# First threshold and goal of the second step on GpSimd, fewer stages in VectorE's bracket update, ties marked once behind the repeat loop

## What is computed

```python
def _adj_from_feats(Xa, W1, W2, W3):
    logits = (Xa @ W1) @ W2 @ (Xa @ W3).T
    idx = jnp.argsort(-logits, axis=1)
    vals = jnp.take_along_axis(logits, idx, axis=1)
    csum = jnp.cumsum(jax.nn.softmax(vals, axis=1), axis=1)
    k_i = jnp.sum(csum < 0.9, axis=1) + 1            # how many are kept
    keep = ...                                       # the k_i largest of each row
    return jax.nn.softmax(jnp.where(keep, logits, -jnp.inf), axis=1)

for s in range(2):                                   # the two steps
    A = _adj_from_feats(Xa, W1, W2, W3)
    Xf, Xb, Xa = Rf @ Xf, Rb @ Xb, A @ Xa
    Z = Z + Xf @ U1[s] + Xb @ U2[s] + Xa @ U3[s]
```

## Time and profile before

| | |
|---|---|
| median of 3 runs | 2055.96 us (2055.61 to 2056.17) |
| the profiled execution | 2057.05 us, of which 2055.3 are its span from first to last instruction |
| busy in the span | TensorE 1783.8 us (87%), VectorE 1666.5 (81%), ScalarE 1365.6 (66%), GpSimd 554.8 (27%) |
| mean granted clock of TensorE | 0.954 of full speed |

### The profile page before, as it was taken

One profiled execution on the slowest core, in us unless ns is written; L12 is line 12 of the kernel. 1 busy time (PEld: TensorE's weight loads), 2 busy tenths in 40 slices (PEclk: granted clock), 3 DMA queues, 4 the chain that ended last, 5 costly groups with the idle time before them and its releaser, 6 DMA issues.

```text
span 2055.3 us, 37644 instructions
## 1 busy us (share of the span) xinstructions
PE 1783.8 (87%) x11660; PEld 1314.4 (64%) x11660; DVE 1666.5 (81%) x4215; ACT 1365.6 (66%) x2157; POOL 554.8 (27%) x869
## 2 busy tenths in 40 slices
PE   3999953899999999994956599999999999999997
PEld 3888831677777777773744366666666666666665
DVE  6444465899999999998871899999999999999996
ACT  5222266788888888883724677777777777777752
POOL 4000030344443444431331032222222222222220
PEclk9999977899999999997978799999999999999999
DMA  6899621444444444442424010101010101010122
GB/s 163 198 203 206 169 99 40 106 114 114 110 103 111 114 106 106 112 111 54 96 50 143 21 40 22 38 24 37 24 37 24 37 24 37 24 37 24 37 89 70
DMA packets 235346, 168.27 MB, mean 82 GB/s; under 512 B 188451, under 2 KB 220577, under 8 KB 235168
## 3 DMA queue, kind: packets, MB, share of 16 engines
q1 hardware_dynamic: 221264, 117.44, 21.1%
q0 software_dynamic: 3744, 22.14, 7.0%
q10 hardware_dynamic: 10288, 28.12, 4.0%
HBM read 107.99 MB, written 37.49 MB: 71 GB/s over the span
## 4 chain that ended last, share of the span: by engine, by line
DVE 46%; PE 19%; DVEq 17%; issue 10%; DMA 3%; ACT 3%; ACTq 0%; POOLq 0%; POOL 0%; SPq 0%
DVE probs_t L1529 7%; DVE stats L1546 5%; DVE stats L1536 5%; DVE window L1426 4%; DVEq L1727 4%; DVE scraps L1426 4%; DVE sorted_e L1555 2%; DVE window L1589 2%; DVEq L1593 2%; DVE expo L1409 2%; DMA probs_t<-astray 2%; DVEq L1553 2%; PE lg L1099 2%; PE bank L1035 2%; PE bank L1034 2%
## 5 line engine op out<-in xcount | busy, mean ns | idle before, releaser
L1122 PE MATMUL bank<-both,s_tile 128*128 128x512 f16 x1352 | 301.6, 380 | 16.1 <-issue 16.1
L1191 PE MATMUL bank<-xcur,probs_t 128*128 128x256 f32 x1352 | 296.1, 379 | 0.0
L1099 PE MATMUL lg<-k_t,q_tile 64*128 64x512 f32 (+1 forms) x820 | 192.9, 572 | 100.3 <-DVE expo L1409 92.0
L1191 PEld LDWEIGHTS bank<-xcur,probs_t 128*128 128x128 f32 x1352 | 254.9, 190 | 33.6
L639 POOL TENSOR_TENSOR window<-window,probs_t 128x832 f16<-128x832 f32 x104 | 223.1, 2145 | 113.4 <-ACT probs_t L876 100.8
L1122 PEld LDWEIGHTS bank<-both,s_tile 128*128 128x128 bf16 x1352 | 132.6, 98 | 165.3 <-issue 18.2
L1409 DVE TENSOR_SCALAR_CACHE_REDUCE expo<-lg 128x1024 f32 (+1 forms) x208 | 205.0, 1022 | 36.5 <-PE lg L1089 16.4
L818 ACT ACTIVATE expo<-expo,neg_max 128x3327 f32<-128x3327 f32 x52 | 159.4, 3066 | 47.0 <-DVE neg_max L1418 47.0
L1099 PEld LDWEIGHTS lg<-k_t,q_tile 64*128 64x128 f32 x820 | 69.9, 194 | 183.4 <-DVE expo L1409 120.1
L665 POOL TENSOR_TENSOR aims<-found 128x2 f32<-128x2 f32 x26 | 5.1, 196 | 623.4 <-ACT found L844 623.4
L839 ACT ACTIVATE turned<-expo,found 128x3327 uint8<-128x3327 f32 x52 | 159.7, 3072 | 3.6
(11 more groups left out here) (295 smaller groups left out, 3643.7 us busy)
## 6 DMA issues: line engine op xcount, KB each, us to landing
s_tile<-s_scratch SPq DMA_DIRECT2D x28, 832.0 KB, 4.5
expo<-in_adj POOLq DMA_DIRECT2D x25, 831.8 KB, 9.5
s_tile<-s_scratch ACTq DMA_DIRECT2D x24, 832.0 KB, 4.5
s_scratch<-s_tile SPq DMA_DIRECT2D x14, 832.0 KB, 9.7
s_scratch<-probs_t SPq DMA_DIRECT2D x6, 832.0 KB, 9.4
s_scratch<-window SPq DMA_DIRECT2D x6, 832.0 KB, 9.4
q_tile<-q_scratch SPq DMA_DIRECT2D x104, 32.0 KB, 2.1
xa_scratch<-ht ACTq DMA_DIRECT2D x26, 128.0 KB, 1.9
```

Of the source, the lines that this page charges most:

```text
L1099: last = T.matmul(lg[c % 2][:, h * CHUNK:h * CHUNK + w], q_tile[b][DA * h:DA * (h + 1), :], k_all[DA * h:DA * (h + 1), s, c0:c0 + w], star ...
L1122: last = T.matmul(s_ps[:, 0:width], s_tile[b][:, k, :], moving, start=(k == 0 and part == 0), stop=(k == NT - 1 and part == 1))
L1191: last = T.matmul(kept_ps[1][:, 0:D], probs_t[:, k * P:(k + 1) * P], xcur[:, k, :], start=(k == 0), stop=(k == NT - 1))
```

## The change

Three things, and sizes of buffers that go with them.

- GpSimd: `first_bracket` goes on to the first cut and its goal. Before, it left the difference of the values and that of the cuts times the upper value. Now it raises the first to the power of -1 (`ALU.pow`), multiplies the second by it, adds the lower end, works out the goal, and multiplies the goal with the four signs of `sides`. `lead` and `mine` get 16 columns for it.
- VectorE, second step: the reciprocal and the product behind L1650 and the goal in `evaluate` are gone. Which ends to replace is decided by comparing `sides` x sum with `sides` x goal, beside the difference rather than behind it. The two instructions of `settle` stand beside the reciprocal's stages; `interpolate` and `settle` are part of `evaluate`.
- VectorE, repeat branch: in the first step the count of ties is taken out of the flag ahead of the loop, the entries equal to the threshold are made ready, and the flags are gathered again, so that the loop runs only if a row is flagged for something else. `take_ties` and `take_above` stand once behind the loop, in both steps.

```diff
@@ -193,8 +193,8 @@
         last_bias = acts[:, 7:8]
         sieved = sb("sieved", [P, 2])
 
-        mine = sb("mine", [P, 12])
-        lead = sb("lead", [P, 2, 12])
+        mine = sb("mine", [P, 16])
+        lead = sb("lead", [P, 2, 16])
         scalar_points = sb("scalar_points", [P, 4])
         aims = sb("aims", [P, 2])
         picked = sb("picked", [P, 2, 8])
@@ -206,14 +206,15 @@
         my_total = mine[:, 4:5]
         my_target = mine[:, 5:6]
         my_slack = mine[:, 6:7]
+        goal = mine[:, 3:4]
         bracket = mine[:, 8:12]
+        goal_by_side = mine[:, 12:16]
         ends_t = sb("ends_t", [P, 4])
         ends_c = sb("ends_c", [P, 4])
         sides = sb("sides", [P, 4])
         which = sb("which", [P, 8], I32)
         reach = sb("reach", [P, 2])
         weight = sb("weight", [P, 1])
-        goal = cells[:, 0:1]
         under = sb("under", [P, 1])
         settled = sb("settled", [P, 1], I32)
         ceiling = sb("ceiling", [P, 1])
@@ -224,6 +225,9 @@
         sorted_e = sb("sorted_e", [P, MOST])
         prefix = sb("prefix", [P, MOST + 1])
         mass = prefix[:, 0:1]
+        row_powers = sb("row_powers", [P, 2])
+        power = row_powers[:, 0:1]
+        below = row_powers[:, 1:2]
         ranks = sb("ranks", [P, 8])
         lists = [sieve[:, HALF - 3 * MOST:HALF], scraps[:, N - N % 4 - 12 * MOST:N - N % 4].bitcast(FP32)]
         equal = rest[:, BEST - 8:BEST]
@@ -239,7 +243,6 @@
         real_row = sb("real_row", [P, 1])
         top = cells[:, 7:8]
         kept = cells[:, 6:7]
-        below = sb("below", [P, 1])
         odd = sb("odd", [P, 32])
         odd_t = rest[:, 0:32]
         odd_q = sb("odd_q", [P, 1])
@@ -578,6 +581,7 @@
             G.memset(parts[:, :, 2 * D:2 * D + 2], 1.0)
             G.memset(zeros_bf[:, :], 0.0)
             G.memset(ceiling[:, :], CEILING)
+            G.memset(power[:, :], -1.0)
             for rank in range(8):
                 G.memset(ranks[:, rank:rank + 1], float(rank))
             for slot, (of_t, of_one, way) in enumerate(((0.0, 0.0, -1.0), (0.9, 0.0, 1.0), (0.0, CEILING, 1.0), (-0.1035, 0.0, -1.0))):
@@ -686,8 +690,16 @@
                     pool.drain()
                 G.tensor_tensor(span[:, :], lead[:, b, 10:12], lead[:, b, 8:10], ALU.subtract)
                 pool.drain()
-                G.tensor_copy(lead[:, b, 2:3], span[:, 1:2])
-                G.tensor_tensor(lead[:, b, 1:2], span[:, 0:1], lead[:, b, 11:12], ALU.mult).then_inc(lead_ready, 1)
+                G.tensor_tensor(span[:, 0:1], span[:, 0:1], lead[:, b, 11:12], ALU.mult)
+                G.tensor_tensor(span[:, 1:2], span[:, 1:2], power[:, :], ALU.pow)
+                pool.drain()
+                G.tensor_tensor(span[:, 0:1], span[:, 0:1], span[:, 1:2], ALU.mult)
+                pool.drain()
+                G.tensor_tensor(lead[:, b, 0:1], span[:, 0:1], lead[:, b, 8:9], ALU.add)
+                pool.drain()
+                G.tensor_scalar(lead[:, b, 3:4], lead[:, b, 0:1], AIM[1], lead[:, b, 6:7], ALU.mult, ALU.add)
+                pool.drain()
+                G.tensor_scalar(lead[:, b, 12:16], sides[:, :], lead[:, b, 3:4], None, ALU.mult).then_inc(lead_ready, 1)
             def centre_result(t, m, b):
                 pool.wait_ge(y_moments, t + 1)
                 y = tile3(y_all, tile_of(m, b))
@@ -1433,36 +1445,26 @@
                                       points[r].rearrange("p (a d) -> p a d", a=1).broadcast_to([P, 2, 2]))
                     dve.drain()
 
-                def interpolate():
-
+                def evaluate(b):
+
+                    mass_under(b, terms)
+                    dve.drain()
+                    V.tensor_tensor(point[:, 1:2], under[:, :], goal, ALU.subtract)
+                    V.scalar_tensor_tensor(out=which[:, 0:4], in0=sides[:, :], scalar=under[:, :], in1=goal_by_side,
+                                           op0=ALU.mult, op1=ALU.is_gt)
+                    dve.drain()
+                    replace_ends(0)
                     V.tensor_tensor(reach[:, :], bracket[:, 2:4], bracket[:, 0:2], ALU.subtract)
+                    V.scalar_tensor_tensor(out=under[:, :], in0=bracket[:, 2:3], scalar=AIM[s], in1=bracket[:, 1:2],
+                                           op0=ALU.mult, op1=ALU.add)
                     dve.drain()
                     V.reciprocal(weight[:, :], reach[:, 1:2])
                     V.tensor_tensor(reach[:, 0:1], reach[:, 0:1], bracket[:, 3:4], ALU.mult)
+                    V.scalar_tensor_tensor(out=settled[:, :], in0=bracket[:, 0:1], scalar=SETTLED, in1=under[:, :],
+                                           op0=ALU.mult, op1=ALU.is_ge)
                     dve.drain()
                     V.scalar_tensor_tensor(out=cut, in0=weight[:, :], scalar=reach[:, 0:1], in1=bracket[:, 0:1],
                                            op0=ALU.mult, op1=ALU.add)
-                    dve.drain()
-
-                def evaluate(b):
-
-                    V.tensor_scalar(goal, cut, AIM[s], my_slack, ALU.mult, ALU.add)
-                    mass_under(b, terms)
-                    dve.drain()
-                    V.tensor_tensor(point[:, 1:2], under[:, :], goal, ALU.subtract)
-                    dve.drain()
-                    V.tensor_scalar(which[:, 0:4], sides[:, :], point[:, 1:2], 0.0, ALU.mult, ALU.is_gt)
-                    dve.drain()
-                    replace_ends(0)
-                    interpolate()
-
-                def settle(b):
-
-                    V.scalar_tensor_tensor(out=weight[:, :], in0=bracket[:, 2:3], scalar=AIM[s], in1=bracket[:, 1:2],
-                                           op0=ALU.mult, op1=ALU.add)
-                    dve.drain()
-                    V.scalar_tensor_tensor(out=settled[:, :], in0=bracket[:, 0:1], scalar=SETTLED, in1=weight[:, :],
-                                           op0=ALU.mult, op1=ALU.is_ge)
                     dve.drain()
                     V.copy_predicated(cut, settled[:, :], bracket[:, 2:3])
                     dve.drain()
@@ -1650,17 +1652,10 @@
                         V.tensor_copy(mine[:, :], lead_of(b))
                     dve.drain()
                     if s == 1:
-                        V.reciprocal(weight[:, :], mine[:, 2:3])
-                        dve.drain()
-                        V.scalar_tensor_tensor(out=cut, in0=weight[:, :], scalar=mine[:, 1:2], in1=bracket[:, 0:1],
-                                               op0=ALU.mult, op1=ALU.add)
                         if not is_last(t):
                             copy_logits(t + 1, other, LOGITS_LATE)
-                        else:
-                            dve.drain()
                     if s == 1:
                         evaluate(b)
-                        settle(b)
                         dve.wait_ge(p_flipped, t * NG + 1)
                     else:
                         few(b)
@@ -1686,13 +1681,20 @@
 
                         dve.drain()
                         V.memset(tries, TRIES)
+                        if s == 0:
+                            V.tensor_tensor(astray[:, :], astray[:, :], tied, ALU.subtract)
+                            V.tensor_scalar(equal, ranks[:, :], tied, below[:, :], ALU.is_lt, ALU.mult)
+                            V.tensor_scalar(least, tied, 8.0, None, ALU.is_gt)
+                            dve.drain()
+                            V.tensor_tensor(astray[:, :], astray[:, :], least, ALU.add)
+                            dve.drain()
+                            find_odd(astray[:, :], t)
+                            dve.reg_load(left, odd_n[0:1, 0:1])
                         with dve.While(left):
                             move_cut(b)
                             rank(b)
                             flag(True)
                             dve.drain()
-                            take_ties(b)
-                            take_above(b, True, 0, N)
                             sum_kept()
                             find_odd(astray[:, :], t)
                             V.tensor_scalar(tries, tries, -1.0, None, ALU.add)
@@ -1701,6 +1703,9 @@
                                                    op1=ALU.mult)
                             dve.drain()
                             dve.reg_load(left, again)
+                        take_ties(b)
+                        take_above(b, True, 0, N)
+                        dve.drain()
                         dve.reg_load(left, odd_n[0:1, 0:1])
                         with dve.While(left):
                             climb(b)
```

## The result

The changed kernel took 2036.36 us (median of 4 runs, 2035.17 to 2037.08) against 2056.07 us of the kernel before beside it: 19.7 us between the medians, and a ratio of 0.9899 with a 95% interval of 0.9883 to 0.9915, which puts the gain at 17.5 to 24.1 us. The forecast was 2028.6 us, 27.4 faster; the time lies inside its range of 2017 to 2051, 7.8 us above its centre. The profiled execution has a span of 2034.7 us, against 2055.3 before, at a granted TensorE clock of 0.958 (mean of the span).

A forecast was written before the change was run, and what follows sets the result against it. VectorE was taken as the second step's bound, TensorE next. From 2057.05 us, 15.2 off for the second step and 12.2 for the repeats gave 2029.65; the runs' median being 1.09 lower, 2028.6, range 2017 to 2051.

The forecast's parts named there:

- three rivals: Cases the range takes in: both repeats real, 0.13; only the number of instructions counts, 0.05; pow of middling length, 0.12.
- The forecast case: Whole kernel: second step 15.2 us and repeats 12.2 us faster, 2018 to 2034 us of its own; chance 0.57.
- middling pow: Second step: pow of 0.7 to 1.4 us holds L1650, keeping only part of the gain, 2034 to 2051 us; chance 0.12.
- five signs of being right: L1180's wait 0.4 us or less, tile distance 33.7, L1650 0.3 to 0.6, repeat only in t=22, t=24 some 12.
- signs of being wrong: A repeat in t=24; VectorE waiting for the bracket each tile, or for late logits; pow over 0.7 us.
- The bound: Second step: VectorE's chain of instructions sets the pace, 34.36 us per tile, with TensorE next, 0.9 us behind.
- Part 3, the repeats: First step's repeat branch: t=22 real, +3.3 us; t=24 flagged for ties alone, -15.5 us; together -12.2 us.
- Part 1, bracket update: VectorE, second step: sides save 0.16 us and settling 0.31 us per tile through fewer drained distances.
- Part 1, taking over: VectorE, L1650 to the next copy of logits: 0.78 us falls to one drained distance of 0.24, saving 0.54 per tile.
- Part 1, goal: VectorE, second step: the goal (L1449) ahead of L1426 goes away, saving 0.12 us per tile.
- Part 2, pow and cover: GpSimd's bracket: +1.5 us, pow up to 0.5, 0.6 to 0.9 of cover left; centring over L1650 loses 0.45 per tile.
- Long pow: GpSimd: pow so long that the bracket becomes the bound, at 2.5 us +25.5, 2081 us; chance 0.10.

The follow-up runs named there:

- fewer stages alone: Kernel before with only interpolate and settle merged, settling's two instructions beside the reciprocal's stages, GpSimd's work as before; 2047.77 us, ratio 0.9958.
- the second pow: Changed kernel with another pow on GpSimd behind the first, its result unused; 2040.59 us, ratio 0.9915.

## Why the prediction was right, and which step of it was not

**How near it came.** The range of 2017 to 2051 holds the time, but it is that wide because it takes in three rivals. The forecast case alone was given 2018 to 2034, and 2036.4 lies above it, in the stretch of middling pow, which didn't happen. So the mechanism is the forecast one and the gain in the second step was put too high. Of the five signs of being right three came (the time of L1652 with the centring beside it, the repeat in t = 22 alone, 12 us in t = 24) and two came halfway (TensorE's wait at 0.50 instead of 0.4 or less, the period at 33.97 instead of 33.7). Of the signs of being wrong none came in full: the bracket is waited for in every second tile, not in each, and the only long row of pow is one that was held.

**The bound: right.** VectorE's chain of small stages set the second step's pace, with TensorE next. Shortening the chain shortened the period, and TensorE's wait for kept_inv shrank, from 0.87 to 0.50 us per tile; 0.4 or less was forecast for a gain of 0.65.

**Part 3, the repeats: right.** -15.3 and +2.3, forecast -15.5 and +3.3. Tile t = 24 was flagged for ties alone and t = 22 for something else, as forecast; which rows it was, no view shows. The microsecond too much has two parts. From L1683 to the loop's first instruction it is 2.85 us (943.39 to 946.24) and not 3.3, since the register load and the branch are 0.5, not 0.8. And the first counting pass of the second ranking took 1.95 us instead of 2.51 (L1531 at 948.38, before L1529 at 942.05); before, an addition of GpSimd (L644, 942.09 to 942.81) lay beside it, and now it was over by then; that this is the cause is likely and not shown. The half microsecond is luck.

**Part 1, bracket update: right.** Sides and settling were to save 0.47, and from L1452 to the second pass 0.50 went away, with both kinds of evidence: the kernel with fewer stages alone has the 0.34 of settling (forecast 0.31) without dropping an instruction, and the three drains put back cost 0.51 where they stand. "VectorE: DVE Perf Modes" of the Trainium skill says in its section on the DRAIN that the next operation does not start until the pipeline is empty, adding that one that isn't held starts earlier, and in "Rules for kernel authors" to minimize the number of operations rather than the semaphores (the prediction put that advice into the first section). For small operations that don't depend on each other the rows here agree with the addition and not with the rule, 0.08 against 0.24 us.

**Part 1, taking over: the step that failed.** "from L1650 to the next copy of logits (L1409) was 0.78 ...; one drained distance of 0.24 is left. Saved 0.54." It is 0.80, so nothing was saved. The two instructions are gone, but two other things took their place:
- The copy takes 0.46 instead of 0.17, because of the centring. The prediction had that as a term of its own, 0.45 lost, and it measured 0.29. "SBUF — State Buffer" of the Trainium skill, section "SBUF: two separate sides", has the lock as its rule; the trace agrees (L706 starts at 1498.17 and ends at 1498.78, L1652 starts at 1498.36 and ends at 1498.82, just behind it). The collision comes in nearly every tile because both instructions follow the bracket: once its cover is gone, GpSimd begins the centring as soon as the bracket is done, and VectorE the copy some 0.15 us later.
- Behind the copy's drain the copy of logits starts 0.34 us later. The price of 0.24 was taken from small instructions; this one's row in the profile has "issue" as its reason. The kernel with the centring moved, where the copy takes only 0.17, has the same 0.34 (L1653 at 1492.90, L1422 at 1493.42), and without the drain 0.13 is left (L1654 at 1492.95 plus 0.18, L1423 at 1493.26). So it belongs to the drain and not to the lock.
Both counted, the step should have read: 0.78 - 0.17 - 0.34 = 0.27 saved, 0.29 of it lost to the lock.

**Part 1, goal: half.** 0.12 forecast, 0.07 measured (neg_max to the first pass 0.18 before, L1418 to L1426, and 0.11 after, L1430 to L1438).

**Part 2, pow and cover: right in kind.** Pow was taken as up to 0.5 us and took 0.57; the long pass catches an earlier stage, as said: L691, one ahead of what it caught before, and in every second tile L689, two ahead. With 0.6 to 0.9 us of cover the forecast had no wait; there is 0.33 in every second tile, 0.16 per tile. The first bracket: +2.0 for the wait, forecast +1.5; most of the rest is pow, 0.57 instead of 0.2. Long pow and middling pow didn't happen. What the second pow cost (0.20 per tile for 0.55) says that the rival was right in that the cover does end there, and that its price, one for one, was too high: it left out that a later long pass catches a later stage.

**The sum per tile:** taking over -0.02, goal 0.07, update 0.50, wait -0.16, together 0.39 saved; the period fell by 0.40. The forecast had 0.65 with 0.45 for the collision in it. Of these terms GpSimd's part has sides 0.16, goal 0.07, taking over -0.02 and wait -0.16, so 0.05, where the run with fewer stages alone says 0.06.

Over the whole second step the gain is 11.4 us, the table's last four rows, where the forecast had 15.2: 3.8 us of the 6.8 by which the profiled span misses its forecast (20.6 instead of 27.4). The repeats gave back 0.8. The rest is **the start**: the first tile of the first step began at 339.99 instead of 336.33. Nothing of the change runs ahead of it but one `memset` of 128 x 1 elements (L584). These are VectorE's rows of the kernel after, and of the kernel with the centring moved, which is the same up to there:

```profile
339.99 0.15 DVE L1648 COPY mine<-found 128x1 f32 x1 [14.99 <-ACT found L864]
```

```profile
336.83 0.15 DVE L1649 COPY mine<-found 128x1 f32 x1 [14.99 <-ACT found L865]
```

So it is no cost of the change: in the 13 profiles here, one of each kernel, the moment lies between 336.3 and 340.0, and among the kernels with the same code up to there it is nearly as wide. The profiled execution before was the earliest of all and that after the latest, so the two spans make the change look worse than it is, by up to 3.7 us. How the medians are hit by this can't be told, since the unprofiled runs have no timeline. Most of it, 2.7 us, is there early: VectorE's first pass over the adjacency matrix, behind the loading of the inputs, starts at 41.19 before and at 43.90 after. What causes it stays open.

## What to carry to other kernels

Where small dependent instructions set the pace, count drained distances and not instructions: here two independent ones behind one drain cost 0.08 us more than one, a drain between them 0.17 on top. A step handed to another engine is free only if it neither comes late nor pushes that engine's wide work onto an instruction of the critical one; here it did both a little, and the move brought nothing that can be measured. When an instruction is deleted, price what is then adjacent (here a drain in front of an instruction that is slow to start), and when a step is delayed inside a loop, look at who needs the last one behind the loop.

## What the runs showed of the hardware

- **The same drain costs differently by what stands behind it.** Between small instructions with fixed operands the drained distance is 0.22 to 0.30 us, 0.07 of it idle. The copy of logits, whose buffer is chosen by the loop's parity at run time, starts 0.34 us after the drained copy has ended, and 0.13 us after it without the drain. Other instructions whose buffer is chosen so behave alike: kept_inv (L1734) has 0.18 of idle time marked "issue" ahead of it, and the second pass at 1507.16 0.17. Tiles 24 and 25 are written out behind the loop, with the same instructions in the same order and fixed buffers, and there the extra time is gone:

```profile
1940.08 0.57 DVE L1652 COPY mine<-lead 128x16 f32<-128x16 f32 x1
1940.75 1.23 DVE L1421 TENSOR_SCALAR_CACHE_REDUCE expo<-lg 128x1024 f32<-128x1024 f32 x1
...
1970.90 0.16 DVE L1734 RECIPROCAL kept_inv<-cells 128x1 f32<-128x1 f32 x1
```

  The copy of logits starts 0.10 us behind the drained copy, and kept_inv 0.07 behind the long pass, which ends at 1970.83. So the address chosen at run time costs 0.24 and 0.11 us behind a drain. No run takes it out inside the loop.
- **GpSimd's pow on 128 x 1 elements takes 0.57 us**, three times a product of the same shape (0.19). A second one behind it takes 0.55.
- **A port lock weighs most on the smallest instructions.** GpSimd's 128 x 2 subtraction takes 3.61 us instead of 0.2 when it starts 0.13 us behind a long two-input pass of VectorE, and once it was pow that was caught, 4.03 us; VectorE's 128 x 16 copy takes 0.46 instead of 0.17 beside the centring.
- **The start of the first step moves by up to 3.7 us from one profile to another**, which is a fifth of this change's whole effect; among kernels with the same code up to there it lies between 336.8 and 340.0.
